# Two attention layers on one core: one transpose for the row maxima, two head groups in one bank, rope neighbours swapped on VectorE

## What is computed

```python
def attention(x, Wq, Wk, Wv, causal):            # layer 0: causal, then @ Wproj; layer 1: neither
    Q, K, V = heads(x @ Wq), heads(x @ Wk), heads(x @ Wv)      # 16 heads of 8 channels
    Q, K = rope(Q), rope(K)                      # x*cos + x_rot*sin; x_rot[2i]=-x[2i+1], x_rot[2i+1]=x[2i]
    s = einsum('bhqd,bhkd->bhqk', Q, K) / sqrt(8)
    return softmax(mask(s) if causal else s) @ V
x = layernorm(x + attention0(x)); x = layernorm(x + moe_ffn(x))
x = layernorm(x + attention1(x)); out = layernorm(x + dense_ffn(x))
```

## Time and profile before

| | us |
|---|---|
| median of 3 runs | 1517.51 |
| lowest, highest | 1498.33, 1526.39 |
| profiled execution: its time | 1522.62 |
| its span, first to last instruction | 1520.9 |
| mean granted TensorE clock | 0.867 |

### The profile page before, as it was taken

One profiled execution on the slowest core, in us unless ns is written; L12 is line 12 of the kernel. 1 busy time (PEld: TensorE's weight loads), 2 busy tenths in 40 slices (PEclk: granted clock), 3 DMA queues, 4 the chain that ended last, 5 costly groups with the idle time before them and its releaser, 6 DMA issues. The chain is left out here.

```text
span 1520.9 us, 24297 instructions
## 1 busy us (share of the span) xinstructions
PE 1267.8 (83%) x8443; PEld 721.0 (47%) x8443; DVE 866.1 (57%) x2600; ACT 864.5 (57%) x1159; POOL 598.5 (39%) x734
## 2 busy tenths in 40 slices
PE   4778788778887596893798898989889968999997
PEld 2334334434443464771343343333344336888885
DVE  4555455556662665446677776677679332434542
ACT  2356556656654662433267776677678635555553
POOL 0353564465333555562303423333331114444543
PEclk9587889889856698896779999799999579999998
DMA  2000000000000402432020000000000000000000
GB/s 81 2 3 2 2 3 3 2 2 3 2 3 1 129 14 57 111 46 61 5 74 2 3 2 3 2 3 2 3 2 3 2 14 7 14 14 14 14 21 14
DMA packets 40312, 28.31 MB, mean 19 GB/s; under 512 B 5184, under 2 KB 34880, under 8 KB 40208
## 3 DMA queue, kind: packets, MB, share of 16 engines
q1 hardware_dynamic: 36192, 23.68, 5.3%
q0 software_dynamic: 3696, 2.76, 1.4%
q10 hardware_dynamic: 320, 0.52, 0.1%
HBM read 15.74 MB, written 8.06 MB: 16 GB/s over the span
## 5 line engine op out<-in xcount | busy, mean ns | idle before, releaser
L467 ACT ACTIVATE a_prob<-a_ps_s 128x1024 f32<-128x1024 f32 (+1 forms) x448 | 426.1, 961 | 165.4 <-PE a_ps_s L615 158.6
L703 DVE TENSOR_REDUCE a_mx<-a_ps_m 128x1 f32<-128x512 f32 x512 | 318.8, 683 | 103.3 <-PE a_ps_m L601 103.2
L633 PE MATMUL a_ps_o<-a_prob,a_vst 128*32 128x256 f32 (+2 forms) x3328 | 303.9, 442 | 43.5 <-ACT a_oT L474 39.5
L601 PE MATMUL a_ps_m<-a_kst,a_qst 24*128 24x512 f32 (+3 forms) x1024 | 302.4, 499 | 13.8 <-DVE a_mx L699 7.6
L699 DVE CUSTOM_DVE_ANT_0 a_junk<-a_ps_m,mask 128x128 f32<-128x128 f32 (+3 forms) x512 | 220.9, 487 | 140.3 <-PE a_ps_m L601 140.0
L615 PE MATMUL a_ps_s<-a_qst,a_kst 26*128 26x512 f32 (+3 forms) x1024 | 241.0, 488 | 31.2 <-ACT a_qst L447 11.0
L615 PEld LDWEIGHTS a_ps_s<-a_qst,a_kst 26*128 26x128 f32 x1024 | 101.9, 208 | 212.7 <-issue 106.6
L362 POOL TENSOR_SCALAR_AFFINE_SELECT a_prob<-a_prob 128x512 f32<-128x512 f32 x128 | 79.8, 636 | 215.9 <-ACT a_prob L467 215.9
L601 PEld LDWEIGHTS a_ps_m<-a_kst,a_qst 24*128 24x128 f32 x1024 | 142.9, 206 | 43.9 <-DVE a_mx L703 18.7
L633 PEld LDWEIGHTS a_ps_o<-a_prob,a_vst 128*32 128x32 f32 x3328 | 72.0, 115 | 151.9 <-issue 99.4
L1793 POOL TENSOR_TENSOR f_hid_lo<-f_gelu_h,f_hid_hi 128x512 fp32r<-128x512 f32 x64 | 83.1, 1298 | 101.3 <-ACT f_hid_hi L1756 101.3
(11 more groups left out here) (297 smaller groups left out, 2182.7 us busy)
## 6 DMA issues: line engine op xcount, KB each, us to landing
f_w<-in_L_ffn_W_dram SPq DMA_DIRECT2D x21, 256.0 KB
a_qst<-a_mrow SPq DMA_DIRECT2D x256, 4.0 KB
x_tiles<-in_L_attn_x_dram SPq DMA_DIRECT2D x8, 256.0 KB, 5.0
normed_rows_dram<-f_nrm SPq DMA_DIRECT2D x8, 256.0 KB, 2.3
f_hT_hi<-expert_sums_dram SPq DMA_DIRECT2D x4, 512.0 KB, 6.2
f1w_h<-in_L_ffn_h_w_dram SPq DMA_DIRECT2D x2, 1024.0 KB, 7.4
f_xin<-x_tiles SPq DMA_DIRECT2D x8, 256.0 KB, 2.3
out_dram<-f_fin SPq DMA_DIRECT2D x8, 256.0 KB, 2.3
```

Source lines behind the costliest of these rows:

```text
L467: act.activation(prob[p % RING][:, h:h + 2, 0:w], ps_s[S_AT["exp", p, u] % SB][:, :, 0:w], ACT.Exp, scale=float(D) ** -0.5).then_inc(s_tak ...
L601: last = pe.matmul(tile[:, c0:c0 + w], qst[r][rows(hh, KEYS), g, P * i:P * i + P], kst[r][rows(hh, KEYS), g, 0:w], start=True, stop=True)
L633: last = pe.matmul(ps_o[VW * hh:VW * hh + VW, q0:q0 + w], vst[b % 2][:, j, HG * g + hh, :], prob[p % RING][:, hh, c0:c0 + w], start=(ph == ...
L703: ins = dve.reduce_max(mx[:, n % 2, i, h:h + 1], tile[:, c0:c0 + w], AX.X)
```

## The change

1. Maxima: `mx` and `mpart` are laid out so that one transpose turns all 32 columns; `mrow` becomes 32 partitions x 128 where it was 8 x 512, and each DMA reads 8 rows of 512 B where it read 2 rows of 2 KB.
2. Values: the values of head groups 0 and 2 fill columns 0 to 8 of a strip of 32, those of groups 1 and 3 columns 16 to 24, the others are zero. So two groups add into `ps_o` one after the other, and `evacuate`, `turn_o`, `norm` run once for a pair of groups (`pair_at`: in the even groups only).
3. Rope: `kt` and `qt` are gone. One `heads` call projects k and q into one tile at f = 2·PH+1; VectorE writes the swapped neighbours with `stream_shuffle` (`swap`), one phase later and behind each half's reductions. GpSimd's rope steps move back by one phase.

```diff
-    F_HEADS = (2 * PH + 1, 2 * PH + 2)
+    F_HEADS = 2 * PH + 1
+    F_ROPE = (2 * PH + 2, 2 * PH + 3)
+    SWAP = [lane ^ NG for lane in range(NG * D)]
...
-    def group_at(p, ph, behind):
+    def pair_at(p, ph):
         n, now = divmod(p, PH)
-        return n + behind if now == ph and 0 <= n + behind < G else None
+        return n // 2 - 1 if now == ph and n % 2 == 0 and 0 < n <= G else None
...
-        mrow = [sbuf(f"mrow{i}", [2 * HG, T]) for i in range(2)]
+        mrow = [sbuf(f"mrow{i}", [2 * HG * QT, P]) for i in range(2)]
...
-                        sp.dma_start(qst[r][row:row + 2, g, :].bitcast(F32), mrow[n % 2][2 * hh:2 * hh + 2, :])\
+                        sp.dma_start(qst[r][row:row + 2, g, :].bitcast(F32), mrow[n % 2][2 * QT * hh:2 * QT * (hh + 1), :])\
...
-                    eng.wait_ge(s_taken, S_AT["heads", b, i] + 1)
+                    eng.wait_ge(s_turned, 2 * b + i + 1)
...
-                            b = batch_at(p, F_HEADS[i] + step // 2, 2)
+                            b = batch_at(p, F_ROPE[i] + step // 2, 2)
...
-                def heads(b, i):
+                def heads(b):
                     if b >= 1:
-                        act.wait_ge(s_rope, ROPE_STEPS * (2 * b - 2 + i) + 2)
-                    filled("heads", b, i)
-                    act.activation(raw[:, i, :, :], ps_s[S_AT["heads", b, i] % SB][:, :, :], ACT.Copy).then_inc(s_taken, 1)
+                        act.wait_ge(s_rope, ROPE_STEPS * (2 * b - 1) + 2)
+                    filled("heads", b)
+                    act.activation(raw[:, :, 0, :], ps_s[S_AT["heads", b] % SB][:, :, :], ACT.Copy).then_inc(s_taken, 1)
...
+                    for r in range(2):
+                        half = slice(H // 2 * r, H // 2 * (r + 1))
+                        ins = act.activation(vst[b % 2][:, :, half, HALF * r:HALF * r + D], src[:, :, half, :], ACT.Copy)
...
                 def evacuate(n):
-                    act.wait_ge(s_pv, (n + 1) * PH)
+                    act.wait_ge(s_pv, 2 * (n + 1) * PH)
...
-                    for turned in range(2):
-                        ins = pe.matmul(tile[:, turned, :], weights["kq"[i] + ("", "t")[turned]][:, :], xT[:, :],
-                                        start=True, stop=True)
+                    for i in range(2):
+                        ins = pe.matmul(tile[:, i, :], weights["kq"[i]][:, :], xT[:, :], start=True, stop=True)
...
-                    for i in range(QT):
-                        last = pe.transpose(bank[0:2 * HG, 0, 0:T // 2].bitcast(BF16)[:, P * i:P * i + P],
-                                            mpart[:, i, :, :].rearrange("p h a -> p (h a)"), identb[:, :])
+                    pe.transpose(bank[0:2 * HG * QT, 0, 0:P // 2].bitcast(BF16),
+                                 mpart[:, :, :, :].rearrange("p h a i -> p (h a i)"), identb[:, :]).then_inc(s_filled, 1)
...
-                        if ph == 0 and n >= 1:
-                            pe.wait_ge(s_oT, n)
+                        if ph == 0 and n % 2 == 0 and n >= 1:
+                            pe.wait_ge(s_oT, n // 2)
...
-                                             prob[p % RING][:, hh, c0:c0 + w], start=(ph == 0 and half == 0),
-                                             stop=(ph == PH - 1), skip_group_check=True)
+                                             prob[p % RING][:, hh, c0:c0 + w], start=(n % 2 == 0 and ph == 0 and half == 0),
+                                             stop=(n % 2 == 1 and ph == PH - 1), skip_group_check=True)
...
+                def swap(b, i):
+                    dve.wait_ge(s_taken, S_AT["heads", b] + 1)
+                    dve.stream_shuffle(raw[:, i, 1, :], raw[:, i, 0, :], SWAP).then_inc(s_turned, 1)
...
-                    dve.memset(st[:, :, :, D + 1:VW], 0.0).then_inc(s_vinit, 1)
-                    dve.memset(st[:, :, :, D:D + 1], 1.0).then_inc(s_vinit, 1)
+                    dve.memset(st[:, :, :, :], 0.0).then_inc(s_vinit, 1)
+                dve.wait_ge(s_vinit, 2)
+                for st in vst:
+                    for r in range(2):
+                        dve.memset(st[:, :, H // 2 * r:H // 2 * (r + 1), HALF * r + D:HALF * r + D + 1], 1.0)\
+                            .then_inc(s_vinit, 1)
...
                 for i in range(2):
+                    swap(0, i)
+                for i in range(2):
                     for step in range(ROPE_STEPS):
                         rope_step(dve, 0, i, step)
+                for i in range(2):
+                    swap(1, i)
...
                             reduce_head(p + LOOK, 2 * half + 1)
+                        if batch_at(p - 1, F_HEADS, 2) is not None:
+                            swap(batch_at(p - 1, F_HEADS, 2), half)
...
                     for g in range(NG):
-                        for t in range(2):
-                            dve.tensor_copy(dst[:, g, :, :, t], heads[:, g, :, :, t])
-                            ins = dve.tensor_copy(other[:, g, :, :, t], heads[:, g, :, :, 1 - t])
+                        ins = dve.tensor_copy(dst[:, g, :, :], heads[:, g, :, :])
```

More of the change, by code:

```diff
@@ L197, in attention @@
         s_slot("xT", b)
-        for i in range(2):
-            s_slot("heads", b, i)
+        s_slot("heads", b)
         if b == 0:
@@ L217, in attention @@
                 s_slot(name, b)
-        for i in range(2):
-            if batch_at(p, F_HEADS[i], 2) is not None:
-                s_slot("heads", batch_at(p, F_HEADS[i], 2), i)
+        if batch_at(p, F_HEADS, 2) is not None:
+            s_slot("heads", batch_at(p, F_HEADS, 2))
         if stacked(p) is not None:
@@ L227, in attention @@
                 m_slot("max", p + LOOK, k)
-        for name, k in (("norm", group_at(p, NORM_AT, -1)),
+        for name, k in (("norm", pair_at(p, NORM_AT)),
                         ("proj", batch_at(p, F_PROJ, -1) if wproj is not None else None)):
@@ L476, in _ @@
                 turn_x(0)
-                for i in range(2):
-                    heads(0, i)
+                heads(0)
                 values(0)
@@ L483, in _ @@
                 turn_x(1)
-                for i in range(2):
-                    heads(1, i)
+                heads(1)
                 turn_maxima(0)
@@ L496, in _ @@
                         turn_x(batch_at(p, F_XT, 2))
-                    for i in range(2):
-                        if batch_at(p, F_HEADS[i], 2) is not None:
-                            heads(batch_at(p, F_HEADS[i], 2), i)
+                    if batch_at(p, F_HEADS, 2) is not None:
+                        heads(batch_at(p, F_HEADS, 2))
                     if stacked(p) is not None:
@@ L639, in _ @@
                 turn_x(0)
-                heads(0, 0)
-                heads(0, 1)
+                heads(0)
                 values(0)
@@ L646, in _ @@
                 turn_x(1)
-                heads(1, 0)
-                heads(1, 1)
+                heads(1)
                 for m in range(LOOK):
@@ L776 @@
 SELECT_STEPS = 4 + 2 * 3 * NG
+HALF = VW // 2
+VINIT = 2 + 4
 I32 = mybir.dt.int32
@@ L2082, in transformer @@
         tables = sbuf("rope_tables", [C, 2, T])
-        heads0, heads1 = [{n: sbuf(f"heads{i}_{n}", [C, C]) for n in ("k", "kt", "q", "qt", "v")} for i in range(2)]
+        heads0, heads1 = [{n: sbuf(f"heads{i}_{n}", [C, C]) for n in ("k", "q", "v")} for i in range(2)]
         x_in = ins["L0_attn_x"].rearrange("b t c -> (b t) c")
```

74 lines of the change are left out of this document (38 added, 36 removed).

## The result

The changed kernel takes 1496.51 us (median of 20 runs, 1489.12 to 1561.71) against 1519.99 for the kernel before, run beside it (20 runs). The ratio is 0.9885, 95% interval [0.9852, 0.9918]: faster by about 1.2%, which is within 2%. The profiled execution has a time of 1498.13 us and a span of 1496.4 (before 1520.9). The forecast of 1457 was too good by 40 us, and 1496.5 lies just above its range.

A forecast was written before the change was run, and what follows sets the result against it. In layer 0's six batches with heads the chain from projection over rope to maxima was taken to set the time, not the matmuls. Terms of -51, -13 and +2.7 gave -61 us, ratio 0.96, 1457 us; range 1420 to 1495.

The forecast's parts named there:

- The sum of -61 us: Whole kernel: -51 us in layer 0, -13 in layer 1, +2.7 for the starts, against the profiled 1522.6 us.
- rival 1: Layer 1: the clock falls there too, behind the new wait at f = 13; +26 us, giving 1483; chance 0.15.
- The two chains: GpSimd's rope and split: layer 0's weigh at f = 12 6.6 us earlier, layer 1's turn at f = 13 2.6 later.
- layer 0's chain: Batches with heads: q's projection goes, GpSimd's split comes earlier, and weigh at f = 12 gets its mask 6.6 us sooner.
- the wait of 3 us for the mask at f = 12: Layer 0: TensorE at f = 12 by 217.5 would wait with weigh for GpSimd's mask until 220.8.
- the 51 us: Layer 0's saving: 6 x (6.6 + 1.2) = 47 us, plus 2 x 2 in the last two batches.
- Layer 1 (+1.8 and -2.9 a batch, -13 in all): Later split +1.8 us, saved evacuations and shorter turns -2.9; six batches -7, last two -3 each.
- The new wait for the split: Layer 1, f = 13: TensorE waits 2 us or more for GpSimd's split, which swaps and two ropes delay.
- Part 2: 32 of 64 evacuations of 0.58 us and 32 turn_o of 0.76 go, with half of 39.5 us of waits.
- Part 3's transpose and the DMAs: Three of four transposes go 64 times, 0.25 us each; the copy takes about 0.3 less; no cost for DMA landing.
- rival 3: Hardly any gain: shorter rows of maxima land 0.7 us later in each of 64 groups, +45, 1502; chance 0.08.
- The starts: Prologue copies give 1.8 us, first swaps and full memsets cost; layer 0 nets 0, layer 1 +2.7.

The follow-up runs named there:

- e7: Changed kernel without the swaps from batch 2 on and with q's rope of layer 1 behind the split: 1448.2 us, 0.9521 of the kernel before.
- e14: Same as e7, with VectorE's shuffles back at their old place, writing a tile nothing reads: 1492.9 us, 0.9802 of the kernel before.
- e9: Changed kernel with swaps and rope steps later and further apart in both layers, nothing left out: 1492.1 us, 0.9791 of the kernel before.
- e3: Changed kernel without the swaps of the batches from 2 on, rope taking stale neighbours: 1487.8 us, 0.9746 of the kernel before.
- e4: Changed kernel with q's rope steps of layer 1 two phases later, behind the split: 1486.6 us, 0.9727 of the kernel before.
- e5: Changed kernel with part 3 in layer 0 alone, q and k projected with both weights in layer 1: 1480.9 us, no ratio.
- e1: Changed kernel with part 3 undone (both projections, no swap), parts 1 and 2 kept: 1503.0 us, 0.9852 of the kernel before.
- e11: Changed kernel with scores issued after maxima and weigh in the first half behind side works with a ScalarE copy: 1515.2 us, 0.9963 of the kernel before.
- e13: Changed kernel with q's rope of layer 1 behind the split and neighbours exchanged by SyncE's DMAs from batch 2: 1541.0 us, 1.011 of the kernel before.

## Why the prediction was wrong

The step that failed is the one that let the clock of before stand. The sum of -61 us has no term for TensorE's clock, and rival 1 priced it for layer 1 alone, at 0.15. The two chains that the sum does work out came as it had them; then 107 us more at 1.2 GHz took some 38 us back. Here are the ends of layer 0's chain, the start before, then the start and the end after; its end before is the last row:

```profile
204.88 1.02 ACT L427 ACTIVATE a_raw<-a_ps_s 128x1024 f32<-128x1024 f32 x1 [1.64 <-PE a_ps_s L615]
...
190.36 1.02 ACT L428 ACTIVATE a_raw<-a_ps_s 128x1024 f32<-128x1024 f32 x1 [1.35 <-PE a_ps_s L536]
...
206.39 1.51 PE L630 MATMUL a_ps_o<-a_prob,a_vst 128*32 128x384 f32 x8
```

- *Layer 0's chain (6.6 us a batch).* It came out to a tenth. From the copy to `raw` to the first `weigh` of f = 12 it was 22.5 us (204.88 to 227.41; 22.5 to 22.8 in five of the six batches) and is 16.0 in each of the six. The turn waits 2.0 us where 2.4 was said and 4.0 stood before. Some luck is in the tenth: the wait of 3 us for the mask at f = 12 did not come. TensorE got there 7.6 us behind the turn and not 4.3, since it ran at 1.2 GHz by then, and the mask was just done. What is missing from the 51 us lies behind this place: a batch of 54.79 us differs from one of 47.61 by the clock alone, so the mean gain is 4.5 us where the steps had 7.8.
- *Layer 1 (+1.8 and -2.9 a batch, -13 in all).* The chain came as said here too: the turn of f = 13 comes 16.04 us behind the copy to `raw` (899.85 to 915.89), where 857.28 to 873.4 had been worked out. The new wait for the split is 8.6 us in six, 1.4 each instead of 2 and more. But the batches became 2.7 us longer. I had counted VectorE's 16 reductions, two swaps and a norm between heads and the turn only as the time at which TensorE gets there, and read VectorE's 223 of 300 us as room where there was none at that place. That they hold TensorE, and that the clock falls behind it, is what e7 and e14 show. As a whole the layer takes 0.7 us more where 10 less was said.
- *Where the miss lies.* Of the 36 us between 61 and the profiled 24.5, some 23 are in layer 0, 11 in layer 1 and 2 in the networks. The experiments explain layer 1. For layer 0 they exclude two causes and find none: e7 has no swaps from batch 2 on, and its batches alternate between 47.6 and 54.8 us as in the changed kernel; e9 has 1.0 us of waits for the split there from 60 to 480 us, and its clock to the end of the layer is still 0.77.
- *Part 2.* Right in total: 32 evacuations of 583 ns, waits for `oT` 20.9 where half of 39.5 was said. They went in layer 1 (18.1 to 3.2 us) and hardly in layer 0 (21.4 to 17.7).
- *Part 3's transpose and the DMAs (rival 3).* The copy is 254 ns where it was 576, and no first scores waited for a DMA in the changed kernel. Rival 3 is refuted.
- *The starts.* The prologue gave 2.7 us instead of 1.8 (the loads of x at 9.26 us, before 11.98); 2.5 of them are left at layer 0's first copy to `raw` (18.03, before 20.48). A memset of 2048 took 1765 ns against 1285: 0.5 each, as said. A swap took 0.73 against my 0.69.
- *The sum.* Spans: the changed kernel's is 24.5 us shorter. Without the 38 us of low clock the gain would have been about 63, near the 61 of the sum. That is an estimate from the rows above, but it says where the error sits: in a term that the forecast held at zero.
- *Rival 1* named the clock in layer 1 and priced it at 26 us. Its price for layer 1 was not far off (61 us more at 0.36 to 0.42, 22 to 26), but it put the cause at the wait of f = 13 alone, and it left out layer 0. e3 shows that this wait can do it (its low stretch begins behind it), e4 that it need not be there: its waits for the split are gone from layer 1, with the clock at 0.81.

What I could have read before: in the earlier trace rows layer 1 spent 958 to 980 at the low clock in one batch of six with no wait of over 1 us in the 15 us ahead of it (the trace of before has 0.80, 0.52 and 0.47 there). That was the sign that the layer stood near the edge, and I had used it only for a price.

The Trainium skill bears on this in two places. "TensorE: Matmul & The Clock Gate", section "A second HAM failure mode: psum-queue depth-cycling", tells of a kernel in which TensorE's short idle times between groups of matmuls, as it cycles through PSUM banks, made the clock go down and up again. The runs here agree: e14 differs from e7 by holds of half a microsecond at `ps_m`, and has a clock of 0.82 where e7 has 0.99. I had weighed only the section on the default state, which led me to look for one long wait. "VectorE: DVE Perf Modes", section "Rules for kernel authors", gives about 2400 ns for a shuffle of 2048 columns, so 600 ns for 512 as an estimate by columns; the row has 732.

What stays open: why layer 0 has more of the low clock in the changed kernel, and why its low stretches alternate between a long and a short one in neighbouring batches; why the low stretches of layer 1 begin where they do once VectorE is not in the way (in e5 behind the stacks, in e1 hardly at all); and why the same holds do not always do it. One batch of e14 stayed at full clock with them, and in e4 three of six low stretches begin earlier, one between 960 and 961 us, where the first held `maxima` starts at 961.44. That the clock falls behind most stretches with holds, and stays up behind the same stretches without them, is what e14 and e7 show for layer 1, and no more.

## What to carry to other kernels

An engine's share over a layer says nothing about slack: look at a stretch between two side works, and compare the engine's work per step with the step itself (here 1.21 against 1.20 us). Work taken off TensorE and put on a neighbour can be paid twice where the neighbour is level with it, once in holds (0.5 us in the batch of e14 that kept the clock) and once in the clock (the rest of its mean of 6.7). Where a forecast adds up chains, it should also have a term for the clock that they leave behind. When one cause is removed and nothing happens, remove two at once before dropping either; and use a change only in the loops where it pays, which gave 5% here where the whole change gave 1.2%.

## What I had not expected of the hardware

- 17.6 us of VectorE's work with no reader cost 45 us of the kernel's time (e7 and e14).
- TensorE's busy time in the profile does not show that it is held: 6.77 against 6.57 of 8 us where the count of matmuls fell from 66 to 51. At the low clock the busy share is even higher (7.98 of 8).
- Filling the waits for copies behind side works with other work (e11) gave 0.9963, where the changed kernel has 0.9817 to 0.9885.
- SyncE needed 4.97 us to issue eight DMAs of 32 KB between SBUF tiles, and TensorE waited up to 4.2 us for the small ones behind them in its order (e13).
